# Four comparisons with a scalar made one comparison of two broadcast operands, in the one-hots of a graph network's edge batches

## What is computed

```python
h = relu(node_features @ node_proj_w.T + node_proj_b)
for l in range(2):
    trans = einsum('nh,tdh->tnd', h, edge_W[l])          # 8 edge types
    msgs  = trans[edge_type, src]
    agg   = segment_sum(msgs, dst, num_segments=num_nodes)
    h     = relu(gru_cell(agg, h, gru_wih[l], gru_whh[l], gru_bih[l], gru_bhh[l]))
out = x + h @ out_w.T + out_b
```

## Time and profile before

| what | value |
|---|---|
| time, median of three runs | 1657.53 us |
| profiled execution, its span from first to last instruction | 2243.1 us |
| TensorE busy | 1624.5 us (72%) |
| VectorE busy | 751.5 us (34%) |
| ScalarE busy | 527.8 us (24%) |
| GpSimd busy | 1201.0 us (54%) |
| granted TensorE clock, mean | 0.846 of full speed |

### The profile page before, as it was taken

One profiled execution on the slowest core, in us unless ns is written; L12 is line 12 of the kernel. 1 busy time (PEld: TensorE's weight loads), 2 busy tenths in 40 slices (PEclk: granted clock), 3 DMA queues, 4 the chain that ended last, 5 costly groups with the idle time before them and its releaser, 6 DMA issues.

```text
span 2243.1 us, 34109 instructions
## 1 busy us (share of the span) xinstructions
PE 1624.5 (72%) x10492; PEld 1125.6 (50%) x10493; DVE 751.5 (34%) x3350; ACT 527.8 (24%) x1268; POOL 1201.0 (54%) x1282
## 2 busy tenths in 40 slices
PE   6468777786867755777775887778787775767776
PEld 4345444444544544556553544545454454555555
DVE  6544332423222243343334122212322223333433
ACT  5132232404233112222211111111413311122221
POOL 6455555555555554544453555555555555555552
PEclk9689898898889877877787899889888987788888
DMA  6324536262543322222222766664243253222221
GB/s 170 102 61 158 155 100 207 71 217 86 179 132 85 99 63 63 67 60 62 60 64 73 234 227 202 204 227 133 67 113 83 71 148 82 63 68 66 64 64 37
DMA packets 183315, 251.55 MB, mean 112 GB/s; under 512 B 24396, under 2 KB 156641, under 8 KB 183201
## 3 DMA queue, kind: packets, MB, share of 16 engines
q0 software_dynamic: 58176, 119.22, 19.3%
q1 hardware_dynamic: 123041, 130.73, 18.5%
q10 hardware_dynamic: 1984, 0.13, 0.1%
HBM read 211.87 MB, written 38.12 MB: 111 GB/s over the span
## 4 chain that ended last, share of the span: by engine, by line
another core or an unknown queue 35%; PE 33%; issue 11%; DVE 10%; ACT 4%; DVEq 3%; DMA 3%; POOL 1%; SPq 0%; ACTq 0%; POOLq 0%
PE ps L1042 9%; PE ps L1113 6%; PE ps L1019 6%; PE ps L1105 4%; PE ps L980 3%; DMA blocks<-node_table 2%; PE ps L1093 2%; DVE acc L1618 2%; DVE onehot L1541 1%; ACT counts L756 1%; DVE acc L1638 1%; ACT sums_sb L822 1%; DVEq L1611 1%; DVE onehot L1576 1%
## 5 line engine op out<-in xcount | busy, mean ns | idle before, releaser
L589 POOL DMA_INDIRECT gath<-node_table,gidx x1212 | 1165.0, 961 | 997.3 <-ACT gidx L627 532.5
L1042 PE MATMUL ps<-counts,blocks 128*128 128x504 f16 (+3 forms) x1764 | 426.1, 388 | 76.1 <-issue 49.6
L1638 DVE TENSOR_TENSOR acc<-ps,acc 128x16 f32 x864 | 151.1, 175 | 901.5 <-remote 364.6
L822 ACT COPY sums_sb<-ps 128x512 f32<-128x512 f32 x216 | 126.5, 586 | 922.9 <-remote 598.4
L1113 PE MATMUL ps<-sums_sb,wT 128*128 128x128 f32 x1728 | 262.1, 315 | 99.9 <-ACT sums_sb L822 81.8
L1019 PE MATMUL ps<-work 128*128 128x392 bf16 x983 | 224.7, 367 | 147.5 <-ACT counts L756 55.4
L1042 PEld LDWEIGHTS ps<-counts,blocks 128*128 128x128 bf16 x1764 | 173.0, 102 | 280.5 <-issue 102.0
L1113 PEld LDWEIGHTS ps<-sums_sb,wT 128*128 128x128 f32 x1728 | 249.7, 227 | 114.3 <-issue 65.5
L1105 PE MATMUL ps<-onehot,gath 128*128 128x128 bf16 x2592 | 204.3, 230 | 62.5 <-issue 37.7
L1093 PE MATMUL ps<-sums_sb,wT 128*128 128x96 f32 (+1 forms) x1408 | 212.9, 310 | 47.4 <-issue 29.7
L1093 PEld LDWEIGHTS ps<-sums_sb,wT 128*128 128x128 f32 x1408 | 202.8, 224 | 71.0 <-issue 57.2
(11 more groups left out here) (198 smaller groups left out, 867.4 us busy)
## 6 DMA issues: line engine op xcount, KB each, us to landing
blocks<-node_table SPq DMA_DIRECT2D x84, 672.0 KB
kept_counts<-counts SPq DMA_DIRECT2D x28, 882.0 KB
counts<-kept_counts SPq DMA_DIRECT2D x28, 882.0 KB
gath<-node_table,gidx POOLq DMA_INDIRECT x1212
node_table<-gath SPq DMA_DIRECT2D x14, 336.0 KB, 3.2
node_table<-work SPq DMA_DIRECT2D x14, 336.0 KB
counts<-in_x_dram SPq DMA_DIRECT2D x1, 3080.0 KB
out_dram<-counts SPq DMA_DIRECT2D x13, 224.0 KB
```

The source lines that it names most:

```text
L589: nc.gpsimd.indirect_dma_start(out=gath[:, b, j, :], out_offset=None, in_=tables[l], in_offset=bass.IndirectOffsetOnAxis(ap=gidx[:, b, j:j ...
L822: act.copy(n_sb[:, b // 2, b % 2 * BG:(b % 2 + 1) * BG, :], narrow_sums[b % 2]) \
L1042: last = nc.tensor.matmul(head_ps[:, 0:COLS[share]], blocks[:, j % 2, at, part * H:(part + 1) * H], counts[:, a, 0:COLS[share]], start=(i ...
L1638: nc.vector.tensor_tensor(win, narrow_ps[q][:, g * NARROW:(g + 1) * NARROW], win, ALU.add) \
```

## The change

The one-hots of a batch come from one `tensor_tensor` over 4 x 192 (or 4 x 128) elements a partition in place of four `tensor_scalar` over 192 (128) each. Its first operand is the number line, repeated over the four groups. Its second is the four codes of the partition, each repeated along its group's row. The operands' types and the values written are the same, and `hot_ready` is raised by that one instruction.

```diff
+                def hots_of(b, batch_codes, codes):
+                    nc.vector.tensor_tensor(
+                        onehot[:, b, :, 0:codes],
+                        iota_b[:, 0:codes].rearrange("p (a c) -> p a c", a=1).to_broadcast([GE, BG, codes]),
+                        batch_codes.rearrange("p (g a) -> p g a", a=1).to_broadcast([GE, BG, codes]),
+                        ALU.is_equal).then_inc(sem_l["hot_ready"], 1)
+
                 def one_hots(group, b):
-                    for j in range(BG):
-                        last = nc.vector.tensor_scalar(onehot[:, b, j, :], iota_b[:], code[:, ds(group + j, 1)], None,
-                                                       ALU.is_equal)
-                    last.then_inc(sem_l["hot_ready"], 1)
+                    hots_of(b, code[:, ds(group, BG)], CODES)
...
                 def narrow_hots(group, b):
-                    for j in range(BG):
-                        last = nc.vector.tensor_scalar(onehot[:, b, j, 0:NCODES], iota_b[:, 0:NCODES],
-                                                       narrow_code[:, ds(group - HEADS[0] + j, 1)], None, ALU.is_equal)
-                    last.then_inc(sem_l["hot_ready"], 1)
+                    hots_of(b, narrow_code[:, ds(group - HEADS[0], BG)], NCODES)
```

## The result

The changed kernel takes 1677.96 us (median of four runs, 1676.35 to 1680.39), the kernel before 1656.82 (four runs): a ratio of 1.0154, interval 1.0129 to 1.0179. It is slower by 21 us, clear of the noise; the forecast was +46, the range 1656 to 1738. Both kernels timed side by side (run after_again) gave 1680.15 against 1647.56, 1.0178 (1.0144 to 1.0212), +33 us.

What follows compares the result with a forecast made beforehand. GpSimd's gathers were taken to bound the kernel (sum 1655.5 us against 1657.5 measured). Holds by the new VectorE instructions, 58 us between 43 and 73, four fifths exposed, added 46 us: 1704 us, range 1656 to 1738.

Steps and rivals of the forecast that it cites:

- GpSimd's queue sets the end: GpSimd's 1212 gathers run almost without a wait when unprofiled, so what lengthens a gather lengthens the kernel.
- the wait-free sum: Gathers laid end to end without waits, with their gaps, head and tail: 1655.5 us, against 1657.5 measured.
- VectorE's own time: One-hots on VectorE: 0.69 us a narrow batch, 0.958 a wide one; net +3 to +12 us, set at zero.
- The law of a hold: A gather starting over 0.055 us into a two-SBUF-operand VectorE instruction loses its remainder less 0.13 us; 43 us in all.
- The signs named for the trace: Gathers' mean 985 to 1005 ns, median near 950, excess over 0.95 us grown from 18.5 to 45 to 70 us.
- The pair as one block: If GpSimd can't get in between a pair's two narrow instructions, they hold it as one of 1.29 us: 73 us in all.
- Rows 12: Trace rows of a gather put as held 3.05 us by wider comparisons without a wait between them; cited for the one-block case.
- Four fifths reach the end: Of 58 us of holds on GpSimd's gathers, four fifths were taken as exposed: +46 us.
- The Trainium skill's inference: A two-input VectorE instruction does not hold up the writing of DMA descriptors; by it 1657.5 us plus nothing.
- A: Rival: gathers are held less, or where GpSimd would have waited anyway, so nothing reaches the end; 1657 us; chance 0.12.
- B: Rival: the VectorE chain, not GpSimd, sets the end; 1661 to 1671 us; chance 0.13.
- C: Rival: runs of comparisons that hold GpSimd are broken up, so the kernel is faster; 1646 us; chance 0.08.

Runs made afterwards that it cites:

- base_two: The kernel before, unedited, run again on a quicker chip: 1647.19 us, ratio 1.0001.
- psum_line: The changed kernel with the number line in PSUM (fp32) in place of SBUF, on a slower chip: 2226.84 us against 2231.59 for the kernel before, 0.9975.
- psum_two: The kernel of psum_line again, on a quicker chip: 1635.74 us against 1646.48 for the kernel before, 0.9936.
- narrow_two: The changed kernel with only narrow batches as one comparison, wide ones four as before, on a quicker chip: 1660.32 us, 1.0072 of the kernel before.
- narrow_only: The kernel of narrow_two on a slower chip: 2221.77 us against 2231.59 for the kernel before, 0.9937.

## Why the prediction was right, point by point

The mechanism and the direction came out as forecast. The size did not: +46 us was forecast, +21 and +33 were measured.

- *GpSimd's queue sets the end.* Right: base_two and the changed kernel show gathers end to end. The step to it was partly luck. It took the wait-free sum of a trace of a slower chip, whose excess happened to be like a quicker chip's, and named the profiler as the cause of the difference.
- *VectorE's own time.* The lengths are right: 686 and 960 ns against 692 and 958. The net of +3 to +12 us is not: the one-hots have 223 us of busy time against 226 in base_two, and VectorE 746.0 against 746.5. Setting it at zero for the end was right; psum_line has the same lengths and loses nothing.
- *The law of a hold (remainder less 0.13 us, from 0.055 us on).* Right at 0.77, 0.47 and 0.30 us in three kernels. The sums were narrow 22 predicted, 20.5 and 23.5 measured; wide 21 predicted, 26.7 and 21.3 measured. That the sums fit so well is in part luck: they assume phases evenly spread, for which there was no row. The signs named for the trace came: a mean of 996 ns with a median of 946, and an excess of 61 us (59 in after_again).
- *The pair as one block, 73 us.* This is the first term that was mis-sized. I took the middle of 43 and 73, and the runs showed the lower end: the longest narrow hold of the changed kernel is 0.60 us (one of 0.89 in after_again) where a block would give up to 1.1. Rows 12 was the wrong neighbour: such long holds are those of runs of comparisons with a scalar. I also gave its hold as 3.05 us, which is the length of its record; the hold is 2.1.
- *What the kernel before already paid.* The second: gathers that start inside its one-hots were held for 6.3 us on a quicker chip. The forecast counted from zero. Net, one-hots add 47 - 6 = 41 us in the changed kernel and 45 - 6 = 39 in after_again, and all gathers together 38 and 36.
- *Four fifths reach the end.* Nearly right where it can be told: 33 of 36 us in after_again. In the first timing only 21 us came of it. Of that chip there is no trace of the kernel before, which took 9 us more there than on the others; where the rest went stays open.
- *The Trainium skill's inference* in "SBUF — State Buffer", "Who interferes with whom", that a two-input instruction does not stall descriptor writing, gave +0. The runs are against it for these gathers. The rule in the same section of the Trainium skill, that an instruction with at most one SBUF input outside the two-port modes does not contend, agrees with psum_two, where none of 159 gathers is held for more than 0.05 us.
- *The rivals.* A is out by the time, B by narrow_two and psum_line. C is out as what decides, but its mechanism is in the traces: the long holds beside the head's comparisons fall by some 5 us (C had put 6), in the changed kernel as well. There the 45 to 47 us of new holds outweigh it; in psum_line it is most of the 8 us by which the gathers are shorter than before.

## What to carry to other kernels

Where GpSimd's indirect gathers set the pace, count a VectorE instruction with two SBUF operands at what it holds GpSimd, not at its own length. Here that was about (length - 0.185)^2 / 2 / 1.25 us, with 1.25 us from gather to gather: 0.24 us for one of 0.96 us (0.24 and 0.30 measured) and 0.10 for one of 0.69 us (0.09 and 0.11 measured). So one long instruction is dearer than several short ones of the same work. Putting one operand in PSUM removed that price here at no cost in length. Before moving anything, look in the trace for an instruction that already has an operand in PSUM, and see what the gathers beside it take. And check that the trace comes from a chip that runs at the timed speed before reading a bound out of it.

## What was not expected

The same kernel takes 1647 or 2231 us by the chip, with a mean granted clock of 0.946 or 0.85, TensorE busy 1431 or 1614 us, and gathers of the same length (965 and 961 ns). A change that costs 0.7% on one kind (narrow_two) gains 0.6% on the other (narrow_only).

A comparison with a scalar that reads 128 fp32 elements from PSUM has a step of 0.27 us on VectorE (232.2 us / 864); the bf16 one from SBUF had 0.18.
